# A new order for mixing, routing and copies inside attention, with 13 unread products on the matmul engine

## The reference, cut to what matters

```
x = x + gate * scans_over_rows_and_columns(gn(x)) ...       # "mixing": gates, two state scans, gelu, tanh
t = tokens(x)                                               # 1024 tokens per image
t = t + attention(ln(t))                                    # 6 heads, window 33 plus one class token
scores = ln(t) @ gate_w + gate_b; keep the best 2 of 4      # "routing"
t = t + sum over kept experts of p_e * (gelu(h @ w1_e) @ w2_e)
```

## Time and profile before

| | |
|---|---|
| median of three runs | 3306.24 us (3303.92 to 3311.53) |
| the profiled execution | 3303.47 us, span 3301.7 us |
| TensorE busy | 2732.3 us (83%) |
| VectorE busy | 1832.3 us (55%) |
| ScalarE busy | 1118.0 us (34%) |
| GpSimd busy | 816.6 us (25%) |
| mean granted TensorE clock | 0.896 of 2.4 GHz |

### The profile page before, as it was taken

One profiled execution on the slowest core, in us unless ns is written; L12 is line 12 of the kernel. 1 busy time (PEld: TensorE's weight loads), 2 busy tenths in 40 slices (PEclk: granted clock), 3 DMA queues, 4 the chain that ended last, 5 costly groups with the idle time before them and its releaser, 6 DMA issues.

```text
span 3301.7 us, 49397 instructions
## 1 busy us (share of the span) xinstructions
PE 2732.3 (83%) x17619; PEld 1970.2 (60%) x17619; DVE 1832.3 (55%) x5182; ACT 1118.0 (34%) x3347; POOL 816.6 (25%) x656
## 2 busy tenths in 40 slices
PE   0467787898988889898988889898988898898497
PEld 0346565666666666666666666666666666665254
DVE  4445454555656565655656565655656565555354
ACT  0023333333333334243333334343333334343122
POOL 0000021232232312232232312232232312232434
PEclk9678887898989899898989899897989899898799
DMA  3330011333232142332233142323232132323465
GB/s 41 93 109 7 19 51 24 88 71 84 66 87 72 38 119 29 106 56 82 66 87 73 38 117 29 110 53 81 66 87 71 36 117 24 94 56 111 122 151 103
DMA packets 272628, 241.72 MB, mean 73 GB/s; under 512 B 209020, under 2 KB 250494, under 8 KB 261760
## 3 DMA queue, kind: packets, MB, share of 16 engines
q1 hardware_dynamic: 211648, 147.17, 16.5%
q0 software_dynamic: 50880, 52.59, 9.6%
q10 hardware_dynamic: 9856, 38.80, 3.7%
HBM read 133.29 MB, written 73.59 MB: 63 GB/s over the span
## 4 chain that ended last, share of the span: by engine, by line
PE 63%; DVE 22%; ACT 5%; issue 4%; POOL 1%; DMA 1%; SPq 1%; DVEq 0%; POOLq 0%; ACTq 0%
PE PSUM L1519 9%; PE PSUM L1496 8%; PE PSUM L1589 7%; PE PSUM L1567 6%; PE PSUM L1537 3%; PE PSUM L1505 3%; PE PSUM L1435 3%; PE PSUM L1539 3%; PE PSUM L1538 3%; DVE HLO L1057 2%; PE PSUM L1391 2%; PE PSUM L1432 2%; PE PSUM L1664 2%; DVE NMX L1108 2%; DVE HHI L1054 2%
## 5 line engine op out<-in xcount | busy, mean ns | idle before, releaser
L841 ACT ACTIVATE PSPT<-PSUM,NMX 94x126 f32<-94x126 f32 x1056 | 366.8, 357 | 685.7 <-PE PSUM L1579 531.9
L1519 PE MATMUL PSUM<-XT,WB 128*128 128x512 f16 x2010 | 523.4, 393 | 52.6 <-DMA META<-slots 52.6
L702 POOL DMA_INDIRECT out_dram<-Y,META x228 | 365.0, 1601 | 596.6 <-DVE Y L1081 470.5
L810 ACT ACTIVATE HF<-PSUM,WB 128x512 f32<-128x512 f32 x402 | 273.8, 685 | 549.1 <-PE PSUM L1519 548.3
L1537 PE MATMUL PSUM<-WB,HHI 128*128 128x192 f16 x1608 | 396.5, 247 | 31.5 <-DVE HLO L1057 30.3
L1539 PE MATMUL PSUM<-WB,HLO 128*128 128x192 f16 x1608 | 395.3, 246 | 0.0
L1538 PE MATMUL PSUM<-WB,HHI 128*128 128x192 f16 x1608 | 395.2, 246 | 0.0
L1567 PE MATMUL PSUM<-KBD,QT 128*94 128x378 f32 x704 | 350.2, 585 | 26.9 <-ACT PSPT L841 25.2
L1054 DVE TENSOR_SCALAR HHI<-HF 128x512 f16<-128x512 f32 x402 | 172.7, 430 | 353.0 <-ACT HF L810 350.5
L1589 PE MATMUL PSUM<-VW,PSPT 126*94 126x32 f32 x2112 | 251.1, 275 | 122.3 <-DVE PSPT L1092 120.9
L1519 PEld LDWEIGHTS PSUM<-XT,WB 128*128 128x128 f16 x2010 | 198.6, 102 | 234.2 <-issue 56.3
(11 more groups left out here) (270 smaller groups left out, 4624.1 us busy)
## 6 DMA issues: line engine op xcount, KB each, us to landing
WB<-weights SPq DMA_DIRECT2D x67, 1600.0 KB, 6.9
XR<-in_x ACTq DMA_DIRECT2D x16, 768.0 KB, 5.3
out_dram<-X ACTq DMA_DIRECT2D x32, 384.0 KB, 3.0
weights<-WB ACTq DMA_DIRECT2D x4, 1600.0 KB, 6.2
GUP<-TGU SPq DMA_DIRECT2D x256, 8.0 KB, 1.8
slots<-XROW,IDX POOLq DMA_INDIRECT x256
out_dram<-Y,META POOLq DMA_INDIRECT x228, 3.6
HF<-in_w ACTq DMA_DIRECT2D x6, 384.0 KB, 5.0
```

The source lines that it names most:

```text
L702: pool.indirect_dma_start(out[:, :], bass.IndirectOffsetOnAxis(row, 0), Y[:, wslot(i, j), q, :], None, bounds_check=B * T + BS - 1, oob_is ...
L810: act.activation(HF[:, k % 2, :], PSUM[:, 4 + k % 2, :], ACT.Gelu, scale=1 / (X_UP * W_UP), bias=bias).then_inc(f["gelu_done"], 1)
L841: e = act.activation(PS[0:QS, n % 2, h, :], PSUM[0:QS, n % 2, h * KS:(h + 1) * KS], ACT.Exp, bias=NMX[:, b, n % 2, h:h + 1], accum_out=DEN ...
L1519: mm = pe.matmul(dst, WB[:, ws, w:w + 128], XT[:, xs, chunk, :], start=(n == 0), stop=(n == 4))
```

## The change

The work is the same; its places differ.

- VectorE, routing: `compare_gates` and the first part of `choose_gates` (now `choose_experts`, up to the winners) move to b = 0, the rest of it (`weigh_experts`) to b = 1, `positions` to b = 2, the first half of `schedule` (now `count_blocks`) to b = 4; the rest of `schedule` stays at b = 5. TensorE's `prefix` moves from b = 3 to b = 1.
- VectorE, attention: the copies of the turned exponentials stand ahead of the first side step, and `normalize` behind the routing piece.
- The side's slots move on all three engines; ScalarE's step comes ahead of an exponential group and no more behind it.
- TensorE gets three unread products at b = 2, 3 and 4, and four at b = 11, ahead of `values`, in all 15 attentions that have side work. They go to bank 6.
- `STEPS`: from chunk 16 on (before: 18) `between` takes three steps per chunk.

```
-        MIX_SLOT = [10, 13, 16, 19]
+        MIX_SLOT = [13, 15, 17, 19]
-        STEPS = [(1, 0) if n < 14 else (1, 1) if n < 18 else (2, 1) for n in range(NSEL * HK)] + [(1, 1)]
+        STEPS = [(1, 0) if n < 14 else (1, 1) if n < 16 else (2, 1) for n in range(NSEL * HK)] + [(1, 1)]
...
# ScalarE, mix: Gelu of H from slot 6 to 10, copy of the turned H from slot 9 to 12
# ScalarE, attention: step(side) ahead of each exponential group
# VectorE, mix
-                    yield from slot.until(tp + 1)
+                    yield from slot.until((0, 1, 4, 6)[tp])
-                yield from slot.until(5)
+                yield from slot.until(8)
-                    yield from slot.until(MIX_SLOT[tp] + 2)
+                    yield from slot.until(MIX_SLOT[tp])
-                    yield from slot.until(MIX_SLOT[tp] + 3)
+                    yield from slot.until(MIX_SLOT[tp] + 1)
# VectorE, attention, after the two maxima
-                    step(side)
+                    if before and b == 0:
+                        compare_gates(i)
+                        choose_experts(i)
                     if b >= 1:
                         copy_turned(2 * b - 2)
                         copy_turned(2 * b - 1)
-                        normalize(b - 1)
+                    step(side)
                     if before and b == 1:
-                        compare_gates(i)
+                        weigh_experts(i)
                     if before and b == 2:
-                        choose_gates(i)
+                        positions(i)
                     if before and b == 4:
-                        positions(i)
+                        count_blocks(i)
                     if before and b == 5:
                         schedule(i)
+                    if b >= 1:
+                        normalize(b - 1)
# TensorE, mix: turn_image(3) from slot 4 to 5, turn of H from slot 8 to 11
# TensorE, attention
                         if not side:
                             keep_busy(8 if b == 1 else 2)
+                        elif 2 <= b <= 4:
+                            pe.wait_ge(s["hs_copied"], at("hs_copied", i + 1, 1))
+                            keep_busy(3, 6)
+                        elif b == NB:
+                            pe.wait_ge(s["mixed"], at("mixed", i + 1, NP))
+                            keep_busy(4, 6)
                         values(2 * b - 2)
                         values(2 * b - 1)
-                    if before and b == 3:
+                    if before and b == 1:
                         prefix(i)
```

More of the change, by code:

```diff
@@ L763, in mix @@
                                ).then_inc(s["hs_copied"], 1)
-                yield from slot.until(6)
+                yield from slot.until(10)
                 act.wait_ge(s["h1_pre"], at("h1_pre", i, 1))
                 act.activation(H1[:], H1[:], ACT.Gelu).then_inc(s["h1_gelu"], 1)
-                yield from slot.until(9)
+                yield from slot.until(12)
                 act.wait_ge(s["h1T_done"], at("h1T_done", i, 1))
@@ L1198, in compare_gates, with choose_experts @@
                 link(dve.tensor_tensor(CMPB[:], mine, other, ALU.is_gt))
-            def choose_gates(i):
-                se, sm1, win = SE[:], SM[:], WIN[:]
-                sm = sm1.unsqueeze(2).broadcast_to((128, NT, E))
+            def choose_experts(i):
+                win = WIN[:]
                 dve.tensor_tensor(CMPA[:], CMPA[:], AFTER[:].unsqueeze(1).broadcast_to((128, NT, E, E)), ALU.mult)
@@ L1209, in choose_gates, with weigh_experts @@
                 dve.tensor_scalar(WINB[:], win, 2.0, None, ALU.is_ge).then_inc(s["winners"], 1)
+            def weigh_experts(i):
+                se, sm1, win = SE[:], SM[:], WIN[:]
+                sm = sm1.unsqueeze(2).broadcast_to((128, NT, E))
                 link(dve.scalar_tensor_tensor(win, win, 2.0, se, ALU.is_ge, ALU.mult))
@@ L1229, in positions, with count_blocks @@
                                          ).then_inc(s["slots_ready"], 1)
-            def schedule(i, last_blocks=False):
-                n, thr = blocks_of(i), THR_ANY if last_blocks else THR_FULL
-                v = 3 if last_blocks else 2
+            def count_blocks(i, last_blocks=False):
+                thr = THR_ANY if last_blocks else THR_FULL
                 dve.wait_ge(s["slots_ready"], at("slots_ready", i, 0))
@@ L1370, in _ @@
             compare_gates(B)
-            choose_gates(B)
+            choose_experts(B)
+            weigh_experts(B)
             positions(B)
+            count_blocks(B, last_blocks=True)
             schedule(B, last_blocks=True)
@@ L1453, in mix @@
                 turn_image(i, 2)
-                yield from slot.until(4)
+                yield from slot.until(5)
                 turn_image(i, 3)
-                yield from slot.until(8)
+                yield from slot.until(11)
                 pe.wait_ge(s["h1_read"], at("h1_read", i, NP))
```

2 lines of the change are left out of this document (added).

## The result

The changed kernel takes 3126.18 us (median of four runs, 3123.61 to 3131.39), the kernel before 3308.89 beside it on the same chip (3303.92 to 3312.79): a ratio of 0.9451, 95% interval [0.9431, 0.947]. Forecast were 3113, between 3045 and 3215. The execution profiled took 3126.97 us.

The account below looks back on a forecast made before the run. Order of work on VectorE, not load, was taken to make TensorE wait and its clock fall. Attentions -200 us, last -4, stages after +11: -193, 3303.47 to 3110, plus 2.8 for the median: 3113; range 3045 to 3215.

Parts of the forecast that it names:

- b = 5: Query block 5: GpSimd's copy collides with the scaling of H, stall 1.4 us (0 to 2.6); iteration 5.7.
- The clock: One clock fall at the stall of query block 5, 2.3 us per image; 1.5 at block 11.
- The products: Unread products at query blocks 2 to 4 lie in a wait for copies; uncovered, up to 2.4 us per image.
- STEPS: Stage after attention: an earlier step lengthens waits, +1.6 us in 13 images; earlier clock return, -0.7 in 14.
- DMA: First token block lands about 1533, first expert product due at 1540.6: hidden, some 7 us to spare.
- Ends: First attention, without routing, 65 us for 73.88; last attention loses its stalls, -4 of 51.39.
- A: Rival: clock holds all the way, no fall at block 5, no loss by step table: 3060 us; chance 0.18.
- B: Rival: one more clock fall per image, in blocks 1 to 4, 70 us more: 3183; chance 0.15.
- C: Rival: tokens come late, SP's queue eats the spare 7 us, 42 us more: 3155; chance 0.05.
- D: Rival: slower, clock stays at 1.2 GHz from block 2 to the end of block 6: 3420; chance 0.04.
- E: Rival: waits only move on VectorE, to blocks 4 and 5, half the gain lost: 3210; chance 0.08.
- fourth view: VectorE's timeline: routing after block 2 delays the maxima (1.00 us) to 1496.70, TensorE stands and the clock falls.

Follow-up runs that it names:

- the order alone: The changed kernel without its 13 unread products and with the old table of steps: 3078.83 us, ratio 0.9326 to the kernel before.
- the early exponential: The order alone, plus one unread ScalarE exponential directly behind the gelu so its table loads early: 3064.71 us, ratio 0.9267 to the kernel before.

## Why the prediction was right

- **The bound.** That order and not load made the waits is confirmed: the order alone, with as many matmuls as before, takes 230 us off (3308.59 to 3078.83). Fifteen attentions came to 1005.90, forecast 1003; an image to 67.5, forecast 67.0.
- **Blocks 0 to 4, 7 to 10.** These took 11.45 us for 12.0, 4.94 for 5.0, 3.83 for 4.0 twice, 17.56 for 18.1, 4.03 for 4.2: all a little under, 1.7 us in sum.
- **b = 5.** The collision came where I put it and at its price (1.4 us ahead of the turns, b = 5 5.95 for 5.7). It hit L1014, not L1015. By the Trainium skill (SBUF — State Buffer, "Who interferes with whom") a VectorE instruction with two SBUF inputs contends with a GpSimd read, one with a single SBUF input or none does not, outside its two-port modes. Three runs agree: 1.90 us for the scaling, 1667 ns for four elements in its place, and nothing lengthened where the copy stood beside PSUM readers.
- **The clock.** One fall came, where I put it, but mis-sized: b = 6 took 10.41 where 6.91 is the price without it, 3.5 us for my 2.3; and at full clock b = 6 itself was 6.91 for my 6.4. That the small terms above made up for these 1.7 us, so that 67.5 met 67.0, is luck. The tail's 1.2 GHz was right: 5.47 for 5.3.
- **The products.** "Lie in a wait" failed at b = 2 (0.42) and held at b = 3 and 4. That they would hold the clock inside attention is not shown anywhere: at b = 2 to 4 it is 1.00 without them. What the thirteen gave, 2.0 us in the stage behind, came with the new table alone. Three at b = 5 gained 36 us.
- **STEPS.** This is the term that failed, in both of its halves. The table was summed at +1.6 in 13 images, 21 us, and cost 27.7. The two waits that I named grew by 1.0 and 0.6, just as summed; the second products' wait for VectorE's split (L1550) grew by 0.8, and I had not counted it. The 0.7 that the tail should return in 14 images, 10 us, hardly showed: with the old table the stages together are 2.1 us shorter than before. So the stages cost 25.6 us for a forecast of 11, and that is the difference of 13 us in the end.
- **DMA.** The last scatter is issued at 1449.00, the first token block from 1454.42 to 1459.75; it has landed at 1465.9 and is needed at 1472.1: 6 us to spare, forecast 7.
- **Ends.** The first attention took 61.55 for 65, the last changed by -6.3 for -4.
- **Rivals.** A fails on the fall, which comes in every image but the first and the last, and on STEPS. B, C and D show nowhere: 1.00 at b = 2 to 4, 6 us to spare on the tokens, full clock at b = 7 to 10. (The argument against D read the old b = 5 as back at 1.00; its row has 0.70.) Of E one wait did move, the 1.4 at b = 5, but not half of the gain went with it.
- **Mechanism less sure than the number.** My fourth view made VectorE's routing the first cause of the stalls. By the runs the mixing steps carry 167 us, routing 15, and those 15 not in the attentions: old routing cost 2.9 us at b = 3 and 4 but relieved b = 5 and 6. The view's chain was one step off as well. At b = 3 it was `values` that waited, for the copies, and not the turns (the 1.43 above). Parts undone one by one (167, 15 and 9) don't sum to 230, so the split is not exact.

## What to carry to other kernels

Where two engines share something, moving the victim one step gave another victim; moving the long instruction beside work that does not touch the shared side gave 56 us. Spend unread matmuls just ahead of the place where the profile shows the clock fall, not along the whole stretch: three at b = 5 did what thirteen elsewhere did not. A step put one earlier in a full stage is paid by every wait it uncovers, so count the waits of all that follow it, not of itself alone. An issue on a queue that has ended is not a block that has landed: read the landing before you call time to spare.

## What was not expected of the hardware

The falls of the clock can come again in the same place in each image: images 8 to 13 of the kernel after have periods (from the start of one attention to the next) of 174.03 to 174.13 us, those of the order alone 170.63 to 170.71. An edit inside such a pattern can be worth nothing (the early exponential: 170.62 in image 7 for 170.63), and one that breaks it can be worth more than its own work: with the old table images 3 to 13 took 167.65 to 173.85, and b = 6 from 6.91 to 11.26. By an estimate from these runs, differences under about 1% between such variants are as much the pattern as the edit: taking the products out gave 26 us with the new table and, by the ratios, nothing with the old one.
